# A causal-attention block on one core: key normalisation, maxima, late tiles and key transfers in other places

## What is computed

```python
x = L0_attn_src                                   # (1, 2048, 128)
x = x + 0.5 * _L0_ffn_ref(_layernorm(x), ...)     # FP4 gate, up and down, blockwise quantised
x = x + _L0_attn_ref(_layernorm(x), ...)          # linear attention, 16 heads of 64, then GELU FFN
x = x + 0.5 * _L0_ffn_ref(_layernorm(x), ...)     # FP4 again
x = x + 0.5 * _L1_ffn_ref(_layernorm(x), ...)     # ReLU FFN, width 512
x = x + _L1_attn_ref(_layernorm(x), ...)          # causal softmax attention, 16 heads
x = x + 0.5 * _L1_ffn_ref(_layernorm(x), ...)
```

## Time and profile before

| | us |
|---|---|
| median of three runs | 1081.2 |
| the profiled execution, its own time | 1089.29 |
| its span in the profile | 1087.5 |
| PE busy | 920.0 |
| DVE busy | 713.5 |
| ACT busy | 513.0 |
| POOL busy | 257.8 |
| first maxima start (PE) | 412.65 |
| first scores start (PE) | 461.85 |

### The profile page before, as it was taken

The page is one execution under the profiler, slowest core; times in us unless marked ns, Lnnn a source line. Parts: engine busy times, 40 slices in busy tenths (PEclk is TensorE's granted clock), DMA queues, the critical chain, the costliest instruction groups (busy, mean ns, idle before and its releaser), DMA issues.

```text
span 1087.5 us, 19966 instructions
## 1 busy us (share of the span) xinstructions
PE 920.0 (85%) x7332; PEld 459.6 (42%) x7353; DVE 713.5 (66%) x1675; ACT 513.0 (47%) x884; POOL 257.8 (24%) x405
## 2 busy tenths in 40 slices
PE   2788888778888687798889899899899989999986
PEld 1444446565676466444323333233322223332225
DVE  7899953468876666775755588566488757676012
ACT  1133332234444232354565556656556656566772
POOL 1546420045554555421311001112000000000000
PEclk9999998999998887988999899999899999999997
DMA  5300000000000040041002300001500000000000
GB/s 183 67 14 1 1 0 1 1 1 1 1 2 1 1 79 10 2 81 20 23 11 58 54 8 24 2 12 35 74 2 11 12 1 15 7 10 5 12 2 10
DMA packets 30935, 23.20 MB, mean 21 GB/s; under 512 B 9609, under 2 KB 27897, under 8 KB 30840
## 3 DMA queue, kind: packets, MB, share of 16 engines
q1 hardware_dynamic: 29928, 21.39, 9.1%
q10 hardware_dynamic: 912, 0.54, 0.2%
HBM read 17.32 MB, written 4.34 MB: 20 GB/s over the span
## 4 chain that ended last, share of the span: by engine, by line
PE 61%; DVE 16%; ACT 7%; POOL 6%; issue 5%; DMA 3%; SPq 1%; ACTq 0%; DVEq 0%; POOLq 0%
PE psum L1677 11%; PE psum L1692 10%; PE psum L1653 7%; DVE arena L1290 5%; PE psum L1618 5%; PE psum L1565 3%; PE psum L1412 3%; PE psum L1371 2%; ACT arena L967 2%; PE psum L1576 2%; PE psum L1534 2%; PE psum L1422 2%; POOL rs L697 2%; DMA arena<-arena 2%; PE psum L1599 2%
## 5 line engine op out<-in xcount | busy, mean ns | idle before, releaser
L1290 DVE TENSOR_REDUCE arena<-psum 128x2 f32<-128x1024 f32 (+2 forms) x320 | 336.3, 1063 | 146.6 <-PE psum L1618 83.2
L967 ACT ACTIVATE arena<-psum 128x1024 f32<-128x1024 f32 (+3 forms) x320 | 286.7, 898 | 169.3 <-PE psum L1653 95.6
L697 POOL TENSOR_TENSOR rs<-ve,mhalf 128x1 f32<-128x1 f32 x128 | 70.7, 559 | 389.3 <-DVE ve L1084 388.8
L1677 PE MATMUL psum<-arena 128*32 128x512 f32 (+3 forms) x1280 | 153.2, 551 | 1.3 <-ACT arena L967 1.3
L1692 PE MATMUL psum<-arena,ones 128*32 128x512 f32 (+3 forms) x1280 | 153.7, 553 | 0.0
L1618 PE MATMUL psum<-arena 48*128 48x512 bf16 (+3 forms) x640 | 114.2, 358 | 25.9 <-ACT arena L967 13.8
L1653 PE MATMUL psum<-arena 50*128 50x512 bf16 (+3 forms) x640 | 116.8, 361 | 11.6 <-DMA arena<-arena 4.0
L1653 PEld LDWEIGHTS psum<-arena 50*128 50x128 bf16 x640 | 31.1, 93 | 200.8 <-issue 135.1
L936 ACT ACTIVATE rh<-psum,fb 128x128 f32<-128x128 f32 x128 | 36.5, 370 | 60.9 <-PE psum L1565 56.9
L803 POOL TENSOR_TENSOR arena<-arena 128x512 f32<-128x512 f32 x15 | 19.1, 1274 | 188.2 <-DMA arena<-scr_sums 188.2
L1371 PE MATMUL psum<-WguT,xqT 128*128 128x352 f32 x128 | 52.1, 536 | 7.0 <-DVE hb L1115 5.8
(11 more groups left out here) (186 smaller groups left out, 1494.9 us busy)
## 6 DMA issues: line engine op xcount, KB each, us to landing
arena<-scr_parts SPq DMA_DIRECT2D x96, 64.0 KB
arena<-scr_sums SPq DMA_DIRECT2D x60, 64.0 KB, 2.0
scr_parts<-arena SPq DMA_DIRECT2D x12, 256.0 KB, 2.6
arena<-arena SPq DMA_DIRECT2D x124, 2.0 KB, 1.7
X<-in_L_attn_src_dram SPq DMA_DIRECT2D x4, 256.0 KB, 4.9
out_dram<-X SPq DMA_DIRECT2D x16, 64.0 KB, 1.6
arena<-in_c_zsel_dram SPq DMA_DIRECT2D x1, 512.0 KB, 3.8
arena<-in_L_attn_Wk_dram SPq DMA_DIRECT2D x1, 512.0 KB
```

The costliest lines, as they stand in the source:

```text
L697: v.tensor_tensor(rs[:, u, t:t + 1], ve[:, u, t:t + 1], mhalf[:, :], ALU.pow).then_inc(s_rstd[u], 1)
L967: v.activation(pr[:, u % RING, pp, :, 0:CH - off], both(("scores", n))[0][:, :, off:CH], ACT.Exp).then_inc(s_p, 1)
L1290: v.tensor_reduce(MXP[:, j, 2 * pp:2 * pp + 2, m], both(("max", g, pp, j, m))[0][:, :, 0:hi - lo], AX_X, ALU.max).then_inc(s_mxd, 1)
L1677: last = mm(bank(O_BANK)[VD * h:VD * h + VD, off:CH], V[kb // TPC][:, kb % TPC, GH * (g % GPC) + h, :], pr[:, u % RING, h // 2, h % 2, 0:C ...
```

## The change

Nothing is computed otherwise; steps stand in other places of the list.

- In the second pass `e_stats` and `e_norm` of the first four tiles stand about half an iteration earlier, while `e_turn` stays.
- Before the first scores stand the maxima of group 0 and four of the eight maxima of group 1. The maxima of all groups are now laid into slots, two to a cell at most in the early groups; a group's `row_max` comes in front of a `scores` step and its `turn_max` behind it. `MAX_LEADS` sets how many cells before the group's first scores: 2 for group 1, 3 for groups 2 to 4, else 4 as before.
- The late tiles 8 to 15 have a start and a pace (`TAIL`): with pace 2 each step of tiles 12 to 15 comes two slots, a cell, behind the one before. Tile 12 waits with its quantisation from before the first scores until slot 2.
- The keys of chunk 1 stand around the first maxima (from slot -9), those of chunks 2 and 3 end a little earlier.
- `store_parts` and `load_queries` of chunks 1 to 3 stand right behind `turn_max` of the third group of the chunk before (groups 2, 6 and 10), where they stood behind the last `split`.

```diff
-SECOND_ORDER = [("d_add", 6, 0), ("add_stats_d", 4, 0), ("quotients0", 0, 0), ("e_norm", 8, 0), ("q0", 0), ("z0", 1),
-                ("e_turn", 8, 0), ("q1", 0), ("e_k", 8, 0), ("x_stats", 0, 0), ("x_turn", 1, 0), ("h_turn", 3, 0),
+SECOND_ORDER = [("d_add", 6, 0), ("add_stats_d", 4, 0), ("e_norm", 8, 1), ("quotients0", 0, 0), ("q0", 0), ("z0", 1),
+                ("e_turn", 8, 0), ("q1", 0), ("x_stats", 0, 0), ("e_k", 8, 0), ("x_turn", 1, 0), ("h_turn", 3, 0),
...
-                ("e_stats", 8, 1), ("den", 0), ("x_stats", 0, 1), ("x_turn", 1, 1), ("d_add", 6, 1),
-                ("e_norm", 8, 1), ("quotients1", 0, 1),
...
+                ("den", 0), ("x_stats", 0, 1), ("x_turn", 1, 1), ("d_add", 6, 1), ("e_stats", 6, 0),
...
-                ("out_norm", 1), ("d_hidden", 5, 1), ("y_add", 2), ("y_norm", 2), ("down", 3, 1),
-                ("e_stats", 6, 0), ("z_turn", 0), ("d_out", 5, 1)]
+                ("out_norm", 1), ("d_hidden", 5, 1), ("e_norm", 6, 0), ("e_stats", 6, 1), ("y_add", 2), ("y_norm", 2),
+                ("down", 3, 1), ("z_turn", 0), ("d_out", 5, 1)]
...
-TAIL_START = {8: -16, 9: -16, 10: -15, 11: -14, 12: -17, 13: -11, 14: -7, 15: -2}
-MAX_START = {0: -16, 1: -8}
-SECOND_KEYS_START, SECOND_KEYS_EVERY = -12, 3
+FIRST_SLOT = -12
+TAIL = {8: (-11, 1), 9: (-11, 1), 10: (-10, 1), 11: (-9, 1), 12: (2, 2), 13: (6, 2), 14: (12, 2), 15: (18, 2)}
+MAX_LEADS = {1: 2, 2: 3, 3: 3, 4: 3}
+SECOND_KEYS_START, SECOND_KEYS_EVERY = -9, 3
...
-                    at = TAIL_START[t] if first else at + gap
+                    at, pace = TAIL[t] if first else (at + pace * gap, pace)
...
-                        if name == "split" and (i - lag) % TPC == TPC - 1:
-                            c = (i - lag) // TPC
-                            out += [("store_parts", c), ("load_queries", c)]
...
-            for g in MAX_START:
+            max_end = [FIRST_SLOT + len(MAXES[0])] + [2 * GROUP_U[g] - 2 * MAX_LEADS.get(g, MAX_LEAD)
+                                                     for g in range(1, MGROUPS)]
+            for g in range(MGROUPS):
+                lo = max_end[g - 1] if g else FIRST_SLOT
                 for k, x in enumerate(MAXES[g]):
-                    slots.setdefault(MAX_START[g] + k, []).insert(0, ("max", *x))
-                slots.setdefault(MAX_START[g] + len(MAXES[g]) - 1, []).extend([("row_max", g), ("turn_max", g)])
+                    slots.setdefault(lo + (max_end[g] - lo) * k // len(MAXES[g]), []).append(("max", *x))
+                slots.setdefault(max_end[g], []).append(("row_max", g))
+                slots.setdefault(max_end[g], []).append(("turn_max", g))
+                if g % GPC == GPC - 2 and g + 2 < MGROUPS:
+                    slots[max_end[g]] += [("store_parts", g // GPC + 1), ("load_queries", g // GPC + 1)]
...
-                lo, hi = GROUP_U[GPC * (c - 2)] + KEYS_START[c], GROUP_U[GPC * c - 1] - MAX_LEAD - KEYS_MARGIN
+                lo, hi = GROUP_U[GPC * (c - 2)] + KEYS_START[c], GROUP_U[GPC * c - 2] - MAX_LEAD
...
                 for i in range(GP):
+                    slot = slots.get(2 * u + i, [])
+                    out += [x for x in slot if x[0] == "row_max"]
                     if u < len(CELLS):
                         out.append(("scores", GP * u + i))
-                    out += maxes[half * i:half * (i + 1)]
+                    out += [x for x in slot if x[0] == "max"]
...
-                    out += others[cut * i:cut * (i + 1)] + slots.get(2 * u + i, [])
+                    out += others[cut * i:cut * (i + 1)] + [x for x in slot if x[0] not in ("row_max", "max")]
```

More of the change, by code:

```diff
@@ L62 @@
                 ("down", 3, 0), ("add_stats_d", 4, 1), ("d_out", 5, 0), ("d_norm", 4, 0), ("z3", 1),
-                ("e_stats", 8, 1), ("den", 0), ("x_stats", 0, 1), ("x_turn", 1, 1), ("d_add", 6, 1),
-                ("e_norm", 8, 1), ("quotients1", 0, 1),
-                ("ff0", 2), ("e_turn", 8, 1), ("den_turn", 0), ("quotients2", 0, 1), ("e_k", 8, 1), ("h_turn", 3, 1),
-                ("quotients3", 0, 1), ("e_v", 8, 1), ("split", 8, 1),
+                ("den", 0), ("x_stats", 0, 1), ("x_turn", 1, 1), ("d_add", 6, 1), ("e_stats", 6, 0),
+                ("quotients1", 0, 1), ("ff0", 2), ("e_turn", 8, 1), ("den_turn", 0), ("quotients2", 0, 1),
+                ("e_k", 8, 1), ("h_turn", 3, 1), ("quotients3", 0, 1), ("e_v", 8, 1), ("split", 8, 1),
                 ("ff1", 2), ("gate_up", 1, 1), ("d_turn", 5, 1), ("out_add", 1), ("d_norm", 4, 1),
-                ("out_norm", 1), ("d_hidden", 5, 1), ("y_add", 2), ("y_norm", 2), ("down", 3, 1),
-                ("e_stats", 6, 0), ("z_turn", 0), ("d_out", 5, 1)]
+                ("out_norm", 1), ("d_hidden", 5, 1), ("e_norm", 6, 0), ("e_stats", 6, 1), ("y_add", 2), ("y_norm", 2),
+                ("down", 3, 1), ("z_turn", 0), ("d_out", 5, 1)]
 EARLY_KEYS = ("e_stats", "e_norm", "e_turn", "e_k", "e_v", "split")
@@ L403, in last_tiles @@
             for t in range(TILES):
-                n, at = TILES + t, None
+                n, at, pace = TILES + t, None, 0
                 for name, gap in TILE_STEPS:
@@ L409, in last_tiles @@
                         continue
+                    if at is None and name == "hidden":
+                        out.append((FIRST_SLOT - 1, (name, n)))
+                        continue
                     first = at is None
-                    at = TAIL_START[t] if first else at + gap
+                    at, pace = TAIL[t] if first else (at + pace * gap, pace)
                     if first or name not in READ_BY.values():
@@ L450, in causal @@
                     put(lo + (hi - lo) * k // len(steps), *x)
-            for g in range(2, MGROUPS):
-                lo, hi = (GROUP_U[g - 1] - MAX_LEAD, GROUP_U[g] - MAX_LEAD)
-                for k, x in enumerate(MAXES[g]):
-                    put(lo + (hi - lo) * k // len(MAXES[g]), "max", *x)
-                put(hi, "row_max", g)
-                put(hi, "turn_max", g)
             for g in range(MGROUPS):
@@ L478, in causal @@
                 here = at.get(u, [])
-                maxes = [x for x in here if x[0] == "max"]
-                half = (len(maxes) + 1) // 2
-                others = [x for x in here if x[0] not in ("max", "row_max", "gelu")]
-                out += [x for x in here if x[0] in ("row_max", "gelu")]
+                others = [x for x in here if x[0] != "gelu"]
+                out += [x for x in here if x[0] == "gelu"]
                 cut = (len(others) + 1) // 2
                 for i in range(GP):
+                    slot = slots.get(2 * u + i, [])
+                    out += [x for x in slot if x[0] == "row_max"]
                     if u < len(CELLS):
                         out.append(("scores", GP * u + i))
-                    out += maxes[half * i:half * (i + 1)]
+                    out += [x for x in slot if x[0] == "max"]
                     if 0 < u <= len(CELLS):
```

1 line of the change is left out of this document (removed).

## The result

The changed kernel takes 1105.3 us (median of four, 1099.85 to 1108.04), the kernel before 1081.1 (now of four, 1079.66 to 1095.3): a ratio of 1.019, 95% interval 1.011 to 1.027. It is slower, beyond the forecast's range of 1055 to 1097; whether by more than 2% the interval leaves open. The ratios in this text leave out runs over 1.5% above the fastest of their kernel and are not quotients of the medians (which would give 1.022 here).

A forecast was written before the change was run, and what follows sets the result against it. PE was taken as the bound, busy 920.0 of 1087.5 us. Terms -9 -8.5 -1 +19 -1 -6.3 +3 +0 = -3.8 gave execution 1085.5; as the profiled run lay 8.1 over the median, 1077.4 us, range 1055 to 1097.

The forecast's parts named there:

- Part 1: Second pass, first keys normalised earlier: PE's waits at `e_turn` mostly go, -9 us, bounds -2.4 and -17.7.
- Part 2: Head of the causal stage, maxima first and late tiles later: idle time leaves, -8.5 us, and -1 for clock.
- -3.1 for the `row_max` waits: Groups 1 and 2: waits of 2.02 and 1.1 us go, as a scores step now stands between.
- Part 3, chunk 1: Moved key transfers: PE waits 15 us at group 4's maxima; with clock and POOL +19, less 1 at group 0's inverse.
- T: PE's start of `turn_max(2)`, from which the landing of chunk 1's loads was counted.
- The 2 us for POOL: Chunk 1: +2 us, as `norm(0)` waits for group 0's inverse, issued behind the keys, with `h_quant2` of tile 29 behind it.
- -4.0 of group 6's maxima: Chunk 2: these maxima are sent ahead of the keys, so PE's wait for them goes, -4.0 us.
- Chunk 2: Wait for group 6's maxima and low clock after it go, -6.3 us; group 5's sums land with the loads, +3.
- The +3: Chunk 2: wait for group 5's sums, whose gather lands with the loads: +3 us, bounds 0 and +7.
- Chunk 3: Loads start at cell 68, not 72, ahead of group 9's gather, which still lands with them: 0, bounds -4 and +4.
- Rival 3: Every small transfer ends up behind the keys, at groups 0, 5 and 9: slower, 1091 us, chance 0.25.
- Rivals 1 and 2: Key loads: fully hidden, 1058 us, chance 0.17; or only their issue counts, a wait of 5, 1066 us, chance 0.13.

The follow-up runs named there:

- e1: Kernel before with only the second pass's `e_stats` and `e_norm` moved earlier: 1071.8 us, ratio 0.989; repeated: 1076.2 us, 0.995.
- e9: Kernel before with the earlier `e_stats` and `e_norm`, and tiles 28 to 31 behind the first scores at two slots a step: 1080.5 us, ratio 0.997.
- c_after: The changed kernel measured once more, unedited, as base for other runs: 1102.7 us, ratio 1.012 to the kernel before.
- e3: Changed kernel with key transfers and key steps of chunks 2 and 3 put back, chunk 1's transfers left moved: 1083.4 us, ratio 1.001.
- e10: Changed kernel with group 4's maxima in cells 12 and 13, not from cell 9 on: 1106.9 us, ratio 1.020.

## Why the prediction was wrong, step by step

**Part 1**, -9: DVE's first maxima came 7.4 us earlier, PE's first matmul for them 5.9 in after and 9.0 in e1. The two iterations with key steps, from one `d_turn` (L1554) to the next iteration's, take 31.8 and 28.7 us and took 37.0 and 34.9. The waits in front of L1584 were to be gone and 4.1 us of them stay, on another DVE step. Right, a little oversized.

**Part 2**, -8.5 and -1: the step that counted half of the head's idle time as gain was wrong. e9 gives it nothing that two traces of part 1 agree on, and nothing in its median. From group 3 to 6 after takes 17 us more than before: what a late tile no longer waits for or computes in front of the first scores it does there. The -3.1 for the `row_max` waits was not tested by itself.

**Part 3, chunk 1**, +19 less 1: the landing was forecast at T + 30.2 to 31.7 and came at T + 31.6. The wait was sized with cells of 13 to 16 us; they took 11.0 (460.59 to 471.56, where the wait begins), less than the 12.00 of the earlier trace rows, so it was 20.6 and not 15, over the upper bound of 18.7. The 2 us for POOL did not come: PE waits for POOL nowhere from 470 to 532. With part 2, and with the -4.0 of group 6's maxima, which also lies ahead of group 6's first exponential, the forecast from the first maxima to group 6 was +4.5, and the traces give +10.6 (201.8 for 191.2). No run separates the missing gain of part 2 from the longer wait in after.

**Chunk 2**, -6.3 and +3: here the forecast failed most. The wait for group 6's maxima went as expected, but from group 5 to 6 it takes 36.6 us as before (36.7), with late tile 31 in it. Group 5's sums cost PE 8.7 us, over the upper end of 7, and half the clock behind them, which had no term. The +3 was taken from group 9's 5.23 and 3.74, a gather behind twelve loads; group 5's in after stands behind 24, and DVE asks for it 2.0 us after its first send. From group 6 to 7 it is +9.7 where +0.7 was forecast (-2.3 and +3).

**Chunk 3**, 0: wrong in the same way. With before's order eight traces take 41.3 to 47.2 us from group 10 to 11, four of them at most 41.7. The profiled run of before, with 47.2, is the longest of these, since its own gather came late. With all loads ahead of the gather, after takes 48.3 and c_after 55.2. I took one long draw for what before always costs, and saw no loss to come.

**The size of the whole error**: the forecast was 1077.4 and the median is 28 us above it. e3 puts chunks 2 and 3 back and takes 11 to 19 us of that away. So the term that failed is the price of the small transfers sent behind the loads: +3 and 0, where e3 and the traces show 11 to 19 us. Rival 3, every small transfer behind the keys, was the right mechanism for them. It was given 1091 and a quarter of the chance, for its terms (+4, +4) came from the same row. Its `norm(0)` did end at T + 36.5, but PE was not held by it. Rivals 1 and 2, hidden loads, fell with 20.6 us.

**The page's rule** that descriptors are consumed in ring order (the Trainium skill, "DMA: Bandwidth & Descriptors", "Queues, rings and completion order") spoke for rival 3. SP's queue agrees with it: in after and c_after the inverse of group 0 and the sums of groups 5 and 9 land 1.4 to 2.3 us behind the last packet of the loads. In ACT's queue the gathers land from 5.0 us ahead of that packet to 2.8 us behind it, so the order in one ring is at most a part of why they are late. I cited the rule and priced the gather from a weaker case all the same.

Open is how the 24 us of the medians divide exactly, since the traces hold single draws of transfers that vary by 8 us, and what makes the packets of one run slower than those of another.

## What to carry to other kernels

Ask of a moved bulk transfer not only who waits for it but which small ones are issued in the 30 us behind it, and when each of those is due; a price from a place with half the bytes ahead, or with a later due time, is too low. A wait that ends last can cover a second one: an edit that removes the first shows nothing alone (e10), so list all readers behind the same queue first. A second queue lets a small transfer be sent ahead of the bulk; that it lands sooner beside it has to be read from landing times, and the engine that issues it pays. An idle stretch filled by postponing work is no gain until the place it goes to has been shown to be idle.
